# Second attention of a six-stage network: score stacks held twice on the two row halves of TensorE, the split of the row maxima rewritten, and a larger share for GpSimd

## The chip, the cores and the metric

One core of one Trainium2 chip runs the whole program in one launch. The metric is the device time of that launch in microseconds (us); smaller is better.

## What is computed

The reference is a network on x of 4 x 1024 tokens with 128 features: half a step of a 4-expert feed-forward, a causal attention, half a step of feed-forward again, half a step of an 8-expert feed-forward, a second attention, and half a step of the 8-expert feed-forward. The change touches the second attention alone. It has 16 heads of 8 features and adds two attentions over the same scores:

```python
S = einsum('bhnd,bhmd->bhnm', Q, K) / dh ** 0.5
W_tau = softmax(S, axis=-1)
W_sigma = 1.0 / ((1.0 + abs(S) / b_) ** 2 + t_ ** 2)
W_sigma = W_sigma / W_sigma.sum(axis=-1)
f = 0.5 * (W_tau @ V) + 0.5 * (W_sigma @ V)
```

In the kernel the sequence has 1024 positions and there are 4 x 16 = 64 pairs of batch and head; "head" below means such a pair. fp32 accuracy of the scores comes from bfloat16 matmuls: q and k are each split in three bfloat16 parts, and products of parts are summed along the contraction.

## The kernel before, in words

The second attention is the function `attend_both`. A head has 8 tiles of 128 rows; a **slot** is two of them (`i` = 0 and 1), so a head has 4 slots (`PER`) and the stage 256. In slot j each engine works on several slots at once, at fixed lags: maxima of slot j, absolute values and squares of slot j-4 (`LS`), exponentials of slots j-6 (`LT`, `LE`), weighting of V for slot j-7 (`LP`). There is no scheduler: the order on each engine is the order in which `body` is written, and semaphores tie the engines together.

Per slot and engine:

- **TensorE (PE)**: for i = 0 and 1 a score tile of 128 x 1024 into `pm`, one into `pb`, one into `pa` (function `scores`, L1442, two matmuls of 512 columns each; K stack and Q stack of 9 products x 8 features = 72 rows, taken as 96 rows, or 128 with the three rows that carry minus the maximum for `pb`). Then `weigh` (L1458): 4 matmuls of 512 columns per tile, side by side on four column groups of 32.
- **VectorE (DVE)**: for each i the row maximum of `pm` (L1604), and clearing the sign bit of `pa` into `sg` (L1612). Then the square step (a + b) * a on columns 800 to 1023 of both tiles (L1628, `scalar_tensor_tensor` with `sg` as both tensor inputs).
- **GpSimd (POOL)**: the same square step on columns 0 to 799 (`CUT` = 25/32 of 1024), in three instructions: the sum for the first 8 columns (`EDGE`, L1397), the sum for the rest (L1399), the product (L1402). It starts when both sign-cleared tiles are there.
- **ScalarE (ACT)**: exp of `pb` twice (L1524), then logarithm (L1539) and exponential (L1543) that turn the square into the sigma weights.

Once per head, in the first slot of the next head (`j % PER == 0`; **head slot** below), DVE also does the **split** (function `part`): the 128 x 8 maxima become three bfloat16 parts of minus the maximum, in five small instructions L1560, L1564, L1567, L1569, L1571, placed between the large ones. PE turns them (L1494), DVE copies them to `rows` one slot later (L1622), SP sends them by DMA into the Q stack (L1418), and `pb` needs them one slot after that. The output of an earlier head (L1583, L1588, L1592) is done in the head slot too. POOL copies `parh` and `Vh` for the next head there (L1386, L1388). SP loads the stacks of the head after the next one in 6 DMAs (`load_stacks`, L974 and L975).

Of the kernel before, what the change touches and what calls it, by code (L numbers as in the profile page):

```python
# [32 lines left out]
RING = 4  # L33
SIGN_OFF = 0x7FFFFFFF
# [1269 lines left out]

def attend_both(nc, tag, V, F, par, qd, kd, ident, stacks, cleared):
# [10 lines left out]
    EDGE = 8  # L1316
    CUT = 25 * T // 32
    with ExitStack() as ctx:
# [29 lines left out]
        HEAD_LOADS = 16 * STACK_DMAS  # L1348
# [22 lines left out]
        with nc.Block() as block:  # L1371

            @block.gpsimd
            def _(pool):
# [3 lines left out]
                def body(it, j):  # L1378
# [4 lines left out]
                    if (j - LS) % PER == 0:  # L1383
                        if some(h, 2):
                            pool.wait_ge(pv_done, PER * (h - 1))
                        nc.gpsimd.tensor_copy(parh[:, ((j - LS) // PER) % RING, :], par[:, h, :])\  # L1386
                            .then_inc(par_ready, 1)
# [13 lines left out]
                    pool.wait_ge(shift_done, 2 * s + 2)  # L1401
# [6 lines left out]
            def _(sp):  # L1408
                sp.wait_ge(cleared, CLEARS)

                def load(h, r, wait):
                    if wait:
                        sp.wait_ge(tau_mm, TT * (h - RING) + TT)
                    load_stacks(sp, Q[r], K[r], qd, kd, h, stack_in[r])
# [22 lines left out]
            def _(pe):  # L1437
                pe.wait_ge(identb_ready, 1)

                def scores(out, lhsT, rhs, t, rows_, sem):  # L1440
                    for lo in range(0, T, CH):
                        last = nc.tensor.matmul(out[:, lo:lo + CH], lhsT[0:rows_, t * P:(t + 1) * P],  # L1442
                                                rhs[0:rows_, lo:lo + CH], start=True, stop=True)
# [20 lines left out]
                def body(it, j):  # L1464
# [325 lines left out]
```

## Time and profile before

| what | value |
|---|---|
| time, median of 3 runs | 3559.43 us (3557.44 to 3564.81) |
| span of the profiled execution | 3560.9 us |
| busy share of the span: PE, DVE, ACT, POOL | 83%, 82%, 69%, 52% |
| the second attention, first to last head (POOL's first and last `parh` copy) | 1476.8 to 3213.3 us |
| granted TensorE clock, mean | 0.911 of full |

The profile gives for the profiled execution its span; no separate time is shown for it, and the span lies within the three runs' times. Busy shares are means over stages with different limits, so the second attention has to be read by itself. In rows of the timeline a duration runs from an instruction's start to its last write, and the next one may start some 0.07 us before that; a start is when the instruction was taken up, not when it got its first data.

### The profile page before, as it was taken

What the parts mean: (1) busy time and instruction counts of PE and PEld (TensorE: products, weight loads), DVE (VectorE), ACT (ScalarE), POOL (GpSimd) and SP (SyncE); (2) the same over time, 40 slices, a digit from 0 to 9 for tenths busy, and PEclk for the clock granted to TensorE, in tenths of its full rate; (3) what the DMA queues carried; (4) which work ended last, traced back from release to release, by engine and by line L of the source; (5) the groups of instructions that cost most, each with busy time, mean ns of one, the idle gap of its engine ahead of it and who ended that gap; (6) DMA issues with size and microseconds to landing.
All of it is one profiled execution on the core that took longest, in us unless ns stands there. A gap on an engine that the chain in (4) does not pass through costs nothing. (4 is left out here: it accounts for less than half of the span.)

```text
span 3560.9 us, 64791 instructions
## 1 busy us (share of the span) xinstructions
PE 2950.8 (83%) x19824; PEld 1285.0 (36%) x19824; DVE 2905.9 (82%) x5109; ACT 2449.7 (69%) x3005; POOL 1854.7 (52%) x1283
## 2 busy tenths in 40 slices
PE   4987999999798897478788788878878888885699
PEld 3753444444576454222222222222222222222455
DVE  5996777777499666699999999999999999997665
ACT  3973656656497453288888888888888888885354
POOL 3210000000121444188888888888888888885354
PEclk9987999999799798699999989998999999897699
DMA  3002111110000000200000000000000000000000
GB/s 88 0 0 99 35 33 33 32 33 25 1 1 0 1 1 0 81 14 11 10 13 10 10 11 13 10 10 12 12 10 11 13 10 10 12 5 1 1 13 12
DMA packets 48969, 62.18 MB, mean 17 GB/s; under 512 B 8464, under 2 KB 27920, under 8 KB 48880
## 3 DMA queue, kind: packets, MB, share of 16 engines
q1 hardware_dynamic: 48880, 61.08, 5.5%
q8 instruction: 45, 0.74, 0.1%
q14 instruction: 44, 0.36, 0.0%
HBM read 45.60 MB, written 14.68 MB: 17 GB/s over the span
## 5 line engine op out<-in xcount | busy, mean ns | idle before, releaser
L1402 POOL TENSOR_TENSOR a_sg<-a_sg,a_shifted 128x1600 f32<-128x1600 f32 x256 | 923.0, 3606 | 21.4
L1524 ACT ACTIVATE a_pt<-a_pb 128x1024 f32<-128x1024 f32 x512 | 526.5, 1028 | 310.0 <-PE a_pb L1442 308.8
L1604 DVE TENSOR_REDUCE a_mx<-a_pm 128x1 f32<-128x1024 f32 x512 | 622.5, 1216 | 89.3 <-PE a_pm L1442 81.6
L1612 DVE TENSOR_SCALAR a_sg<-a_pa 128x1024 int32<-128x1024 int32 x512 | 617.3, 1206 | 29.0 <-PE a_pa L1442 28.3
L1287 DVE TENSOR_REDUCE a_mx<-a_pm 128x1 f32<-128x512 f32 (+3 forms) x768 | 404.0, 550 | 158.6 <-PE a_pm L1126 150.4
L1458 PE MATMUL a_po<-a_pt,a_Vh 128*32 128x512 f32 x2048 | 527.8, 639 | 2.2 <-ACT a_sg L1543 2.2
L1458 PE MATMUL a_po<-a_sg,a_Vh 128*32 128x512 f32 x2048 | 527.7, 639 | 0.0
L1214 ACT ACTIVATE a_pt<-a_pb 128x512 f32<-128x512 f32 (+3 forms) x768 | 337.2, 501 | 268.6 <-PE a_pb L1140 96.4
L1539 ACT ACTIVATE a_sg<-a_sg,a_parh 128x2048 f32<-128x2048 f32 x256 | 514.0, 2008 | 0.0
L1543 ACT ACTIVATE a_sg<-a_sg 128x2048 f32<-128x2048 f32 x256 | 492.5, 1924 | 0.0
L1399 POOL TENSOR_SCALAR a_shifted<-a_sg,a_parh 128x1584 f32<-128x1584 f32 x256 | 453.4, 1771 | 0.1
L1442 PE MATMUL a_pm<-all_K,all_Q 96*128 96x512 bf16 x1024 | 345.4, 422 | 129.0 <-DVE a_mx L1604 111.9
L1442 PE MATMUL a_pa<-all_Q,all_K 96*128 96x512 bf16 x1024 | 341.6, 418 | 41.2 <-DVE a_sg L1612 28.9
L1442 PE MATMUL a_pb<-all_Q,all_K 128*128 128x512 bf16 x1024 | 342.2, 418 | 8.2 <-ACT a_pt L1524 8.2
L1071 POOL COPY a_Vh<-all_V 128x72 f32 (+1 forms) x64 | 13.9, 252 | 567.9 <-PE a_po L1158 567.9
L1123 PE MATMUL a_pm<-all_K,all_Q 96*128 96x512 bf16 (+3 forms) x768 | 258.5, 342 | 24.6 <-DMA all_K<-k_parts 21.4
L1137 PE MATMUL a_pb<-all_Q,all_K 128*128 128x512 bf16 (+3 forms) x768 | 247.1, 327 | 7.9 <-ACT a_pt L1214 7.4
L1628 DVE SCALAR_TENSOR_TENSOR a_sg<-a_sg,a_parh 128x448 f32<-128x448 f32 x256 | 222.1, 867 | 8.9
L1158 PE MATMUL a_po<-a_pt,a_Vh 128*32 128x512 f32 (+3 forms) x1536 | 224.1, 497 | 0.0
L614 ACT ACTIVATE f_sg<-f_psg 128x512 f32<-128x512 f32 x176 | 105.1, 597 | 167.9 <-PE f_psg L573 166.9
L1397 POOL TENSOR_TENSOR a_shifted<-a_sg,a_parh 128x16 f32<-128x16 f32 x256 | 75.9, 297 | 272.6 <-DVE a_sg L1612 247.7
L327 POOL TENSOR_TENSOR f_hidl<-f_hid,f_hidh 128x512 f16<-128x512 f32 x64 | 76.3, 1193 | 263.3 <-ACT f_hid L398 263.3
(244 smaller groups left out, 6061.9 us busy)
## 6 DMA issues: line engine op xcount, KB each, us to landing
all_Q<-q_parts SPq DMA_DIRECT2D x384, 48.0 KB
all_K<-k_parts SPq DMA_DIRECT2D x384, 48.0 KB
q_parts<-p_parts SPq DMA_DIRECT2D x16, 384.0 KB, 2.6
k_parts<-p_parts SPq DMA_DIRECT2D x16, 384.0 KB, 2.6
all_Q<-a_rows SPq DMA_DIRECT2D x128, 6.0 KB
out_dram<-all_X SPq DMA_DIRECT2D x8, 256.0 KB, 2.3
sw_raw<-in_f_We_dram SPq DMA_DIRECT2D x1, 1024.0 KB, 7.1
sw_raw<-in_f_w_gP_dram SPq DMA_DIRECT2D x1, 704.0 KB, 11.0
```

The source lines that it names most:

```text
L1123: last = nc.tensor.matmul(out[:, 0:hi - lo], Q[r][0:96, t * P:(t + 1) * P], K[r][0:96, lo:hi], start=True, stop=not diagonal)
L1214: nc.scalar.activation(pt[:, u, t % 2, lo:hi], pb[:, y % 3, lo % CH:CH], ACT.Exp, scale=SC)\
L1287: nc.vector.tensor_reduce(mx[:, j % 2, half, u, t:t + 1], pm[:, y % 3, 0:min(CH, (t + 1) * P - half * CH)], AX.X, ALU.max).then_inc(max_re ...
L1399: nc.gpsimd.tensor_scalar(shifted[:, :, EDGE:CUT], buf[:, :, EDGE:CUT], b2, 1.0, ALU.add, ALU.mult)\
L1402: nc.gpsimd.tensor_tensor(buf[:, :, 0:CUT], buf[:, :, 0:CUT], shifted[:], ALU.mult)\
L1442: last = nc.tensor.matmul(out[:, lo:lo + CH], lhsT[0:rows_, t * P:(t + 1) * P], rhs[0:rows_, lo:lo + CH], start=True, stop=True)
L1458: last = nc.tensor.matmul(po[32 * q:32 * q + 32, :], Vh[:, ((j - LP) // PER) % 2, t, :], wts[:, i, half * CH:(half + 1) * CH], start=(t == ...
L1524: nc.scalar.activation(pt[(j - LT) % 4][:, i, :], pb[:], ACT.Exp, scale=SC)\
L1539: nc.scalar.activation(buf[:], buf[:], ACT.Ln, bias=parh[:, ((j - LE) // PER) % RING, 1:2]).then_inc(ln_done, 1)
L1543: nc.scalar.activation(buf[:], buf[:], ACT.Exp, scale=-1.0).then_inc(sig_done, 1)
L1604: nc.vector.tensor_reduce(mx[:, (j // PER) % 2, t:t + 1], pm[:], AX.X, ALU.max)\
L1612: nc.vector.tensor_scalar(sg[(j - LS) % 4][:, i, :].bitcast(I32), pa[:].bitcast(I32), SIGN_OFF, None, ALU.bitwise_and).then_inc(abs_done, 1)
```

## The change

- Both operands of the scores are held twice, on partitions 0 to 50 and 64 to 114. Six products of parts are kept instead of nine (48 rows, and 3 more for the maxima: 51). The two matmuls of a score tile (columns 0 to 511, 512 to 1023) read the two copies, so that they lie on different row halves of the array.
- The loads of a head are 12 DMAs instead of 6, and the maxima are sent by 2 DMAs instead of 1. The rows of ones are set by two memsets on POOL in the stage before (`load_sharpness`).
- The split is four `tensor_tensor` instructions with both inputs in SBUF. The maxima are now taken negated, so the sign is not changed in the split. The fifth place is empty.
- `CUT` goes from 25/32 to 27/32; the `EDGE` instruction on POOL is gone, and a nop carries POOL's wait for the sign-cleared tiles. `parh` is copied one head ahead.

```diff
+HALF = P // 2
+QPARTS = (0, 0, 0, 1, 1, 2)
+PAIRS = len(QPARTS) * DH
+MAX_ROW = PAIRS
...
+def load_halves(eng, Q, K, qd, kd, g, sem):
+
+    for base in (0, HALF):
+        row = base
+        for part, times in ((0, 3), (1, 2), (2, 1)):
+            rows = slice(row, row + times * DH)
+            eng.dma_start(Q[rows, :], qd[part, g].unsqueeze(0).broadcast_to([times, DH, T])).then_inc(sem, 16)
+            eng.dma_start(K[rows, :], kd[0:times, g]).then_inc(sem, 16)
+            row += times * DH
...
+def set_ones(eng, Ks, sem):
+
+    for base in (0, HALF):
+        eng.memset(Ks[base + 32:base + HALF, 0:RING, :], 1.0).then_inc(sem, 1)
...
-    EDGE = 8
-    CUT = 25 * T // 32
+    CUT = 27 * T // 32
...
                     if some(s):
                         pool.wait_ge(sq_pool, s)
+                    pool.wait_ge(par_ready, h + 1)
                     pool.wait_ge(abs_done, 2 * s + 2)
-                    pool.wait_ge(par_ready, h + 1)
+                    pool.nop(nofuse=True)
...
-                    nc.gpsimd.tensor_tensor(shifted[:, :, 0:EDGE], buf[:, :, 0:EDGE],
-                                            b2.unsqueeze(2).broadcast_to([P, 2, EDGE]), ALU.add).then_inc(shift_done, 1)
-                    nc.gpsimd.tensor_scalar(shifted[:, :, EDGE:CUT], buf[:, :, EDGE:CUT], b2, 1.0, ALU.add, ALU.mult)\
+                    nc.gpsimd.tensor_scalar(shifted[:], buf[:, :, 0:CUT], b2, 1.0, ALU.add, ALU.mult)\
                         .then_inc(shift_done, 1)
...
                     sp.wait_ge(rows_sb, h + 1)
-                    sp.dma_start(Q[r][ONES_ROW:ONES_ROW + SPLIT, :].rearrange("s (t n) -> s t n", n=P),
-                                 rows[:]).then_inc(rows_in[r], 16)
+                    for base in (0, HALF):
+                        sp.dma_start(Q[r][base + MAX_ROW:base + MAX_ROW + SPLIT, :]
+                                     .rearrange("s (t n) -> s t n", n=P), rows[:]).then_inc(rows_in[r], 16)
...
                 def scores(out, lhsT, rhs, t, rows_, sem):
-                    for lo in range(0, T, CH):
-                        last = nc.tensor.matmul(out[:, lo:lo + CH], lhsT[0:rows_, t * P:(t + 1) * P],
-                                                rhs[0:rows_, lo:lo + CH], start=True, stop=True)
+                    for base, lo in ((0, 0), (HALF, CH)):
+                        last = nc.tensor.matmul(out[:, lo:lo + CH], lhsT[base:base + rows_, t * P:(t + 1) * P],
+                                                rhs[base:base + rows_, lo:lo + CH], start=True, stop=True)
                     last.then_inc(sem, 1)
...
-                        nc.vector.tensor_scalar(neg3[:, 0, :], top, -1.0, None, ALU.mult).then_inc(chain, 1)
-                    else:
-                        dve.wait_ge(chain, 4 * h + n)
+                        nc.vector.tensor_tensor(neg3[:, 0, :], low, low, ALU.max).then_inc(chain, 1)
                     if n == 1:
-                        nc.vector.scalar_tensor_tensor(rem[:], top, -1.0, neg3[:, 0, :], ALU.mult, ALU.subtract)\
-                            .then_inc(chain, 1)
+                        dve.wait_ge(chain, 3 * h + 1)
+                        nc.vector.tensor_tensor(neg3[:, 1, :], low, neg3[:, 0, :], ALU.subtract).then_inc(chain, 1)
                     if n == 2:
-                        nc.vector.tensor_copy(neg3[:, 1, :], rem[:]).then_inc(chain, 1)
+                        nc.vector.tensor_tensor(rem[:], low, neg3[:, 0, :], ALU.subtract).then_inc(chain, 1)
                     if n == 3:
-                        nc.vector.tensor_tensor(rem[:], rem[:], neg3[:, 1, :], ALU.subtract).then_inc(chain, 1)
-                    if n == 4:
-                        nc.vector.tensor_copy(neg3[:, 2, :], rem[:]).then_inc(parts_ready, 1)
+                        dve.wait_ge(chain, 3 * h + 3)
+                        nc.vector.tensor_tensor(neg3[:, 2, :], rem[:], neg3[:, 1, :], ALU.subtract)\
+                            .then_inc(parts_ready, 1)
...
-                            nc.vector.tensor_reduce(mx[:, (j // PER) % 2, t:t + 1], pm[:], AX.X, ALU.max)\
-                                .then_inc(max_red, 1)
+                            nc.vector.tensor_reduce(mx[:, (j // PER) % 2, t:t + 1], pm[:], AX.X, ALU.max,
+                                                    negate=True).then_inc(max_red, 1)
```

DVE's order in the head slot, in the steady part of the stage, of the kernel before (`a_neg` and `a_rem` are the tiles of the split, `a_mx` the maxima, `a_sg` the absolute scores; the first row ends the slot before):

```order
L1628 SCALAR_TENSOR_TENSOR a_sg<-a_sg,a_parh 128x2x224
L1560 TENSOR_SCALAR a_neg<-a_mx 128x8
L1604 TENSOR_REDUCE a_mx<-a_pm 128x1
L1564 SCALAR_TENSOR_TENSOR a_rem<-a_mx,a_neg 128x8
L1583 RECIPROCAL a_rz<-a_ptr 128x16
L1612 TENSOR_SCALAR a_sg<-a_pa 128x1024
L1567 CAST a_neg<-a_rem 128x8
L1588 TENSOR_TENSOR a_fw<-a_ptr,a_rz 128x128
L1604 TENSOR_REDUCE a_mx<-a_pm 128x1
L1569 TENSOR_TENSOR a_rem<-a_rem,a_neg 128x8
L1592 TENSOR_TENSOR all_XNT<-a_fw 128x8x8
L1612 TENSOR_SCALAR a_sg<-a_pa 128x1024
```

And the same place on DVE in the changed kernel:

```order
L1652 SCALAR_TENSOR_TENSOR a_sg<-a_sg,a_parh 128x2x160
L1586 TENSOR_TENSOR a_neg<-a_mx 128x8
L1628 TENSOR_REDUCE a_mx<-a_pm 128x1
L1589 TENSOR_TENSOR a_neg<-a_mx,a_neg 128x8
L1607 RECIPROCAL a_rz<-a_ptr 128x16
L1636 TENSOR_SCALAR a_sg<-a_pa 128x1024
L1591 TENSOR_TENSOR a_rem<-a_mx,a_neg 128x8
L1612 TENSOR_TENSOR a_fw<-a_ptr,a_rz 128x128
L1628 TENSOR_REDUCE a_mx<-a_pm 128x1
L1594 TENSOR_TENSOR a_neg<-a_rem,a_neg 128x8
L1616 TENSOR_TENSOR all_XNT<-a_fw 128x8x8
L1636 TENSOR_SCALAR a_sg<-a_pa 128x1024
```

The four small instructions stand where the first four stood; the fifth is gone from before the next square step.

POOL's order in one slot in the loop, of the kernel before:

```order
L1392 REGISTER_ALU
L1393 ISA
L1397 TENSOR_TENSOR a_shifted<-a_sg,a_parh 128x2x8
L1399 TENSOR_SCALAR a_shifted<-a_sg,a_parh 128x2x792
L1402 TENSOR_TENSOR a_sg<-a_sg,a_shifted 128x2x800
```

And in the changed kernel:

```order
L1426 REGISTER_ALU
L1427 TENSOR_TENSOR a_sg<-a_sg,a_shifted 128x2x864
L1420 ISA
L1424 TENSOR_SCALAR a_shifted<-a_sg,a_parh 128x1728
L1426 REGISTER_ALU
```

POOL's large sum now follows its waits directly, with no short instruction ahead of it.

## Rows read from the trace of the kernel before

**Rows 1.** Stretch, us; busy PE, PEld, DVE, ACT, POOL (instructions); clock; DMA; GB/s
```profile
1800.00:2400.00 600.00, 487.76 (x2590) 139.03 (x2578) 562.72 (x644) 502.93 (x376) 505.70 (x311) 0.92 0.04 11
```
**Rows 2.** The `parh` copies, one per head: all of them by line, then three in time
```profile
L1386 POOL COPY a_parh<-all_par x64: 174/180/199, 1476.8 to 3213.3; 128x2 f32 x60, 128x2 f32<-128x2 f32 x4
...
2397.63 0.18 POOL L1386 COPY a_parh<-all_par 128x2 f32 x1
...
2425.78 0.18 POOL L1386 COPY a_parh<-all_par 128x2 f32 x1
...
2452.30 0.18 POOL L1386 COPY a_parh<-all_par 128x2 f32 x1
```
**Rows 3.** Timeline, DVE at a head boundary: start us, duration us, instruction
```profile
2445.79 1.22 DVE L1628 SCALAR_TENSOR_TENSOR a_sg<-a_sg,a_parh 128x448 f32<-128x448 f32 x1
2446.94 0.18 DVE L1560 TENSOR_SCALAR a_neg<-a_mx 128x8 bf16<-128x8 f32 x1
2447.07 1.23 DVE L1604 TENSOR_REDUCE a_mx<-a_pm 128x1 f32<-128x1024 f32 x1
2448.21 0.46 DVE L1564 SCALAR_TENSOR_TENSOR a_rem<-a_mx,a_neg 128x8 f32<-128x8 f32 x1
...
2448.76 1.16 DVE L1612 TENSOR_SCALAR a_sg<-a_pa 128x1024 int32<-128x1024 int32 x1
2449.84 2.55 DVE L1567 CAST a_neg<-a_rem 128x8 bf16<-128x8 f32 x1
...
2452.50 1.21 DVE L1604 TENSOR_REDUCE a_mx<-a_pm 128x1 f32<-128x1024 f32 x1
...
2455.08 0.74 DVE L1628 SCALAR_TENSOR_TENSOR a_sg<-a_sg,a_parh 128x448 f32<-128x448 f32 x1
```
**Rows 4.** Timeline, POOL over the same stretch
```profile
2442.92 3.61 POOL L1402 TENSOR_TENSOR a_sg<-a_sg,a_shifted 128x1600 f32<-128x1600 f32 x1
2446.76 0.34 POOL L1397 TENSOR_TENSOR a_shifted<-a_sg,a_parh 128x16 f32<-128x16 f32 x1 [0.23 <-POOL a_sg L1402]
2447.07 1.58 POOL L1399 TENSOR_SCALAR a_shifted<-a_sg,a_parh 128x1584 f32<-128x1584 f32 x1
2448.74 3.62 POOL L1402 TENSOR_TENSOR a_sg<-a_sg,a_shifted 128x1600 f32<-128x1600 f32 x1
...
2455.13 0.22 POOL L1397 TENSOR_TENSOR a_shifted<-a_sg,a_parh 128x16 f32<-128x16 f32 x1 [2.46 <-DVE a_sg L1612]
2455.32 1.95 POOL L1399 TENSOR_SCALAR a_shifted<-a_sg,a_parh 128x1584 f32<-128x1584 f32 x1
```
**Rows 5.** Timeline, the stage after the attention: DVE
```profile
3284.45 2.32 DVE L937 TENSOR_TENSOR o_t<-o_rs 128x8 f32<-128x8 f32 x1
3286.80 2.26 DVE L938 TENSOR_TENSOR o_t<-o_t,o_ve 128x8 f32<-128x8 f32 x1
```
**Rows 6.** Timeline, the same stretch: POOL
```profile
3283.47 3.27 POOL L902 TENSOR_TENSOR o_y<-o_y,all_lw 128x1024 f32<-128x1024 f32 x1 [2.96 <-DVE o_y L942]
3286.70 2.33 POOL L898 TENSOR_TENSOR all_X<-all_X,all_lb 128x1024 f32<-128x1024 f32 x1
```
**Rows 7.** PE alone, two stretches: us, PE busy, granted clock, DMA share, GB/s
```profile
2402.50:2409.30 6.80, 6.71 (x25) 0.54 0.07 23
2409.30:2425.80 16.50, 14.68 (x87) 1.00 0.03 9
```
**Rows 8.** Timeline, PE at the lower clock: first and last group of one slot's weighing
```profile
2405.27 1.06 PE L1458 MATMUL a_po<-a_pt,a_Vh 128*32 128x512 f32 x2
...
2407.83 1.06 PE L1458 MATMUL a_po<-a_pt,a_Vh 128*32 128x512 f32 x2
```
**Rows 9.** SP issuing one head's six loads: the first and the last
```profile
2404.93 0.76 SPq L974 DMA_DIRECT2D all_Q<-q_parts  x1
...
2409.36 0.73 SPq L975 DMA_DIRECT2D all_K<-k_parts  x1
```
**Rows 10.** POOL's earlier memset of ones, by line: duration ns min/median/max
```profile
L986 POOL MEMSET all_K<- x1: 6924/6924/6924, 25.2 to 25.2; 32x8192 bf16 x1
```

More of the change, by code:

```diff
@@ L1347, in attend_both @@
             m.sem(x) for x in ("taumm", "tauexp", "vh", "par", "pv", "osb", "oturned", "fd", "rz", "weighed"))
-        HEAD_LOADS = 16 * STACK_DMAS
+        HEAD_LOADS = 16 * HALVES_DMAS
         def at(it, j, lag):
@@ L1385, in body @@
                             pool.wait_ge(pv_done, PER * (h - 1))
-                        nc.gpsimd.tensor_copy(parh[:, ((j - LS) // PER) % RING, :], par[:, h, :])\
-                            .then_inc(par_ready, 1)
+                        if not some(h):
+                            nc.gpsimd.tensor_copy(parh[:, 0, :], par[:, h, :]).then_inc(par_ready, 1)
+                        if not (isinstance(h, int) and h + 1 >= HEADS):
+                            nc.gpsimd.tensor_copy(parh[:, ((j - LS) // PER + 1) % RING, :], par[:, h + 1, :])\
+                                .then_inc(par_ready, 1)
                         nc.gpsimd.tensor_copy(Vh[:, ((j - LS) // PER) % 2, :, 0:DH + 1], V[:, h, :, :])\
@@ L1408, in _ @@
             def _(sp):
-                sp.wait_ge(cleared, CLEARS)
+                sp.wait_ge(cleared, CLEARS + 2)
                 def load(h, r, wait):
@@ L1469, in body @@
                     if st is not None and (j - LT) % PER == 0:
-                        pe.wait_ge(rows_in[rt], 16 * (it + (j - LT) // PER // RING + 1))
+                        pe.wait_ge(rows_in[rt], 32 * (it + (j - LT) // PER // RING + 1))
                     for i in range(2):
@@ L1474, in body @@
                                 pe.wait_ge(max_red, 2 * sm + i)
-                            scores(pm, Q[rm], K[rm], 2 * (j % PER) + i, 96, max_mm)
+                            scores(pm, Q[rm], K[rm], 2 * (j % PER) + i, PAIRS, max_mm)
                         if st is not None:
@@ L1478, in body @@
                                 pe.wait_ge(tau_exp, 2 * st + i)
-                            scores(pb, K[rt], Q[rt], 2 * ((j - LT) % PER) + i, P, tau_mm)
+                            scores(pb, K[rt], Q[rt], 2 * ((j - LT) % PER) + i, PAIRS + SPLIT, tau_mm)
                         if ss is not None:
@@ L1482, in body @@
                                 pe.wait_ge(abs_done, 2 * ss + i)
-                            scores(pa, K[rs], Q[rs], 2 * ((j - LS) % PER) + i, 96, abs_mm)
+                            scores(pa, K[rs], Q[rs], 2 * ((j - LS) % PER) + i, PAIRS, abs_mm)
                         if i and sp_ is not None:
@@ L1554, in part @@
                         return
-                    h, top = head(it, j, 1), mx[:, ((j - 1) // PER) % 2, :]
+                    h, low = head(it, j, 1), mx[:, ((j - 1) // PER) % 2, :]
                     if n == 0:
@@ L1619, in body @@
                             if some(h):
-                                dve.wait_ge(rows_in[r], 16 * (it + ((j - 2) // PER - 1) // RING + 1))
+                                dve.wait_ge(rows_in[r], 32 * (it + ((j - 2) // PER - 1) // RING + 1))
                             nc.vector.tensor_copy(rows[:], ptr[:].bitcast(BF16)[0:SPLIT * TT, 0:P])\
@@ L1633, in attend_both, with load_sharpness @@
         m.clear_sems()
-def load_sharpness(nc, tag, par, beta, t):
+def load_sharpness(nc, tag, par, beta, t, Ks, ones_set):
     with ExitStack() as ctx:
@@ L1643, in load_sharpness, with _ @@
         with nc.Block() as block:
+            @block.gpsimd
+            def _(pool):
+                set_ones(pool, Ks, ones_set)
             @block.sync
@@ L1736, in program @@
             lambda: ln_transposed(nc, "n5", X, XNT, ident, add_to_x=True),
-            lambda: load_sharpness(nc, "s5", par, layer["a1_"]["beta"], layer["a1_"]["t"]),
+            lambda: load_sharpness(nc, "s5", par, layer["a1_"]["beta"], layer["a1_"]["t"], stacks[1], cleared),
             lambda: project(nc, "p5", XNT, V, qd, kd, a1, a1_in, True, 2.0),
```

5 lines of the change are left out of this document (3 added, 2 removed).

## The prediction

> **What bounds the kernel now.** I read the windows first, then the copies that mark the heads, then the timeline of a head boundary, since the change is all in the second attention and most of it happens once per head. In the middle of that stage DVE is busy 562.7 of 600 us, PE 488, ACT 503, POOL 506 [rows 1]: no engine is full. The `parh` copies give the pitch of a head: (3213.3 - 1476.8) / 63 = 27.56 us, and single heads take either 28.15 us or 26.5 us (2397.63 to 2425.78, 2425.78 to 2452.30) [rows 2]. POOL's two large instructions need 3.61 + 1.58 us per slot when nothing holds them [rows 4], so with the gaps some 23 of the 26.5 us; the rest is lost at the head boundary. The reader should see in [rows 3, 4] that **DVE and POOL hold each other up**. A DVE instruction with two SBUF tensors as inputs, or a cast from SBUF to SBUF, is not done while a POOL instruction runs; whichever comes second waits for the whole of the other:
>
> - L1628 starts at 2445.79 under L1402, which ends at 2446.53; it ends at 2447.01, 0.48 later, though a free one takes 0.74 [rows 3, 4].
> - L1564 (8 columns, two inputs) takes 0.46 us and ends 0.02 us after L1399. The cast L1567 starts at 2449.84 and ends at 2452.39, 0.03 us after L1402 [rows 3, 4]: 2.4 us lost, per head.
> - The other way round, L1399 takes 1.95 instead of 1.58 us when L1628 has started just before it [rows 4].
>
> While DVE waits in the cast, POOL runs dry for 2.46 us, since its next tile needs both L1612 of that slot [rows 4]. In the other slots POOL's pitch is L1402 end to L1402 end: 2446.53 to 2452.36, 5.83 us, in which L1628 and L1397 take the 0.54 us between 2446.53 and 2447.07. So POOL and DVE in turn set the end; PE does so only while its clock is at 1.2 GHz.
>
> **The change, part by part.** I count from the end of POOL's product before the boundary (0 = 2446.53).
>
> *Split.* This kind of instruction stands in the next stage: `tensor_tensor` on 128 x 8 fp32, L937 with the same tile as both inputs, L938 with two. They take 2.32 and 2.26 us [rows 5], and end 0.03 us after POOL's L902 and L898 [rows 6]. So the new instructions are held up like the cast. There is more: L937 gets through between two POOL instructions because it was already waiting; L938, taken up at 3286.80, just after L898 (3286.70), waits for all of it. Now the first instruction of the split. Before, the short L1397 stood ahead of L1399: L1560 (taken up at 0.41) waited for it and went in ahead of L1399, done at 0.59 [rows 3, 4]. Now L1628 (320 instead of 448 columns, 128 / 448 of 0.467 us less, taken from its 0.48 after release) ends at 0.35, the first split instruction is taken up at 0.28, and POOL's sum stands ready at 0.23, where L1397 stood. I take it that POOL goes first.
>
> *POOL.* The product scales with columns: 3.61 x 27 / 25 = 3.89. The sum: 1.58 x 1728 / 1584 = 1.72. L1397 goes. Pitch in a plain slot: 0.23 + 1.72 + 0.09 + 3.89 = 5.93 (before 5.83).
>
> *The head slot, now.* POOL: sum 0.23 to 1.95, product 2.04 to 5.93. DVE: first split instruction done at 1.98; maximum from 1.93; second split instruction taken up 1.14 later, at 3.07, waits for the product, done at 5.96. From there the distances of [rows 3], with the reciprocal between: sign clearing 6.05, third split instruction 7.13 (POOL is dry, no wait), second maximum 7.40 (before 2452.50, which is 5.97), square step 2.58 after that (2452.50 to 2455.08), at 9.98 (before 8.55). POOL's sum ends 2.20 after that at 12.18 (before 2.19: 2455.08 to 2457.27), its product at 12.27 + 3.89 = 16.16. Two plain slots: 16.16 + 2 x 5.93 = **28.02 us per head**. DVE keeps up in these: from one square step to the next it needs 0.6 and four large instructions at 1.1 to 1.2, 5.2 us; with the copy of `rows` 5.4.
>
> *PE.* Before, at a clock of 0.54, the head takes 28.15 instead of 26.5 [rows 2, 7]; PE had been idle while DVE stood in the cast. Half of the score columns now run beside the other half, so the six pairs of a slot cost the time of six matmuls instead of twelve; at 2.4 GHz this was hidden behind POOL and stays hidden. At 1.2 GHz 512 columns are 0.43 us, and the four groups of weighing, 0.85 apart, 3.4 [rows 8]: a slot needs 6 x 0.43 + 3.4 = 6.0 instead of 12 x 0.43 + 3.4 = 8.6 us, against POOL's 5.93. Between 0 and 1.7 us per head I take 0.2, near the lower end, since DVE and ACT have slack after the head slot.
>
> *Edits with nothing to pay.* SP has 12 loads at 0.88 (2404.93 to 2409.36 is five steps) = 10.6 us instead of 5.3, and one more row DMA of 0.9 [rows 9], of 28 us; the loads are for the head after the next. The second row DMA comes some 1 us later at `pb`; PE's slack per slot covers it. ACT is busy 503 of 600 us [rows 1], 23.1 per head. If POOL did not cover, each would show as a wait of under 1 us.
>
> *Ones.* The memsets write 2 x 4096 columns; 8192 took 6.92 us [rows 10]. The stage before lasts about 6 us, so up to 3.5 us are added; I take 3.
>
> **Sum:** 64 x (28.02 + 0.2 - 27.56) = 42, and 3: +45 us on the span of 3560.9 or the median of 3559.4, which differ by less than the runs do. **3605 us.**
>
> The Trainium skill ("VectorE: DVE Perf Modes", section "Mode 2×_2P") says that the mode with both read ports is for instructions with one source, and that `tensor_tensor` cannot use it. Read by itself it would let the split escape from POOL, and the time would be that of the first rival below, 3400 instead of 3605. Its page "SBUF — State Buffer", section "Who interferes with whom", has the other half, two SBUF inputs against a POOL instruction that reads; with that one the trace agrees, at 2.32 and 2.26 us for an instruction of 128 x 8. "TensorEngine Tiling (Array Packing)", section "Key Properties", says that a change of tiling mode drains TensorE; no row prices it.
>
> **The rivals.**
>
> 1. *The two-input form is not held up.* Then neither the 1.5 nor the 2.7 us of waiting arise, and DVE never falls behind: 4 x 5.93 = 23.7, with POOL's two copies at the boundary and small losses 25 us per head, 64 x 2.5 = 160 us less, 3400. Against it: [rows 5, 6], at the same shape. For it: nothing here. 7%.
> 2. *The first split instruction gets in ahead of POOL's sum*, because POOL's own taking up costs 0.1 us more than at L1397. Then it is done at 0.4, the maximum runs 0.35 to 1.5, the second slips in between sum and product (as L1564 did), and the third waits for the product as the cast did. The end is as before plus POOL's columns: 26.53 + 4 x 0.12 = 27.0 us, and the low clock costs less than before (27.0 to 27.5): 64 x (-0.56 to -0.06) + 3 = 3526 to 3558. It is decided by 0.1 us between two starts. 20%.
> 3. *PE at the lower clock for long stretches*, since it has less to do and longer gaps. A slot is then the chain pair, maximum, sign clearing, pair, weighing: 0.63 + 1.2 + 1.2 + 0.43 + 3.4 = 6.9 us, and with the 2.7 us of waiting at the boundary 30.3 us per head if the clock stays low all the time, 3738; half the time, some 3670. For: the clock falls behind each gap [rows 7]. Against: it comes back within 7 us. 13%.
>
> The forecast, all held up, 3580 to 3640, has 60%.
>
> **How the numbers follow.** The range 3525 to 3670 takes in the forecast, nearly all of rival 2 and the lower part of rival 3. A measurement of this kernel can tell about 0.2%, 7 us. Faster: rival 1 and most of 2, 25%. Same: 8%. Slower: 67%.
>
> **What would show it.** In the changed profile: the first split instruction about 1.7 us long and ending with POOL's sum, the second about 2.9 us and ending with POOL's product, third and fourth 0.15 us; POOL idle some 4 us per head ahead of its sum; the square step on DVE some 1.3 us in the other slots; `parh` copies 28.2 us apart. Short split instructions, or a first one of 0.2 us, would prove rival 1 or 2; a granted clock well under 0.9 rival 3.

## The result, and the profile after

The changed kernel takes **3597.24 us** (3593.86 to 3601.18, 4 runs) against 3561.51 (3557.44 to 3564.81, 4 runs) for the kernel before: a ratio of 1.010, 95% interval 1.0088 to 1.0112. It is slower by 36 us; forecast were 3605, that is +45. The span of the profiled execution is 3599.4 us, 38.5 more than before. The size fits; the way to it does not. I begin with the windows, in the middle of the second attention (columns as in [rows 1]):

```profile
1800.00:2400.00 600.00, 439.93 (x2531) 100.11 (x2533) 549.69 (x607) 495.70 (x369) 503.06 (x217) 0.80 0.05 15
```

PE does its work in 440 us instead of 488, and its granted clock has gone from 0.92 to 0.80 [rows 1]. Every engine is less busy than before, and none is full.

Next the `parh` copies, by line, then five in time (compare [rows 2]):

```profile
L1412 POOL COPY a_parh<-all_par x63: 176/184/204, 1479.3 to 3225.4; 128x2 f32 x60, 128x2 f32<-128x2 f32 x3
...
2366.38 0.19 POOL L1412 COPY a_parh<-all_par 128x2 f32 x1
2395.98 0.18 POOL L1412 COPY a_parh<-all_par 128x2 f32 x1
2425.34 0.18 POOL L1412 COPY a_parh<-all_par 128x2 f32 x1
2452.47 0.18 POOL L1412 COPY a_parh<-all_par 128x2 f32 x1
2479.60 0.18 POOL L1412 COPY a_parh<-all_par 128x2 f32 x1
```

These four heads take 29.60, 29.36, 27.13 and 27.13 us. Of the 61 steady heads 43 lie at 27.0 to 27.2 and 18 between 28.2 and 29.8; their mean is (3225.4 - 1533.1) / 61 = 27.74, where 1533.1 is the second copy. The kernel before, counted from its second copy at 1533.5 in the same way, has (3213.3 - 1533.5) / 62 = 27.09. The difference, 0.65 x 61 = 40 us, is the whole of the 38.5. All of what the mean has above the short heads (27.10 on average) comes from the 18 long ones. In the kernel before, 42 heads take up to 27.15 us (26.57 on average) and 20 take 28.0 to 28.3.

Which form does the head take? The four split instructions, by line (duration ns min/median/max, first and last start):

```profile
L1586 DVE TENSOR_TENSOR a_neg<-a_mx x64: 152/177/1568, 1503.9 to 3249.2; 128x8 bf16<-128x8 f32 x64
...
L1589 DVE TENSOR_TENSOR a_neg<-a_mx,a_neg x64: 156/467/3473, 1505.8 to 3249.4; 128x8 bf16<-128x8 f32 x64
...
L1591 DVE TENSOR_TENSOR a_rem<-a_mx,a_neg x64: 142/2794/2803, 1507.0 to 3252.1; 128x8 f32<-128x8 f32 x64
...
L1594 DVE TENSOR_TENSOR a_neg<-a_rem,a_neg x64: 147/150/153, 1508.2 to 3255.0; 128x8 bf16<-128x8 f32 x64
```

I had forecast 1.7, 2.9, 0.15 and 0.15 us. The first takes 0.15 to 0.18 in 62 of 64 heads. In 44 heads the second takes 0.47 (but for one) and the third 2.8: the pattern of my second rival. In 19 others the second takes 2.3 to 3.5, as I had it for the second, and the third 0.14 to 0.15. First the more frequent form, in the head of 27.13 us that ends at 2479.60; DVE (compare [rows 3]):

```profile
2472.76 1.33 DVE L1652 SCALAR_TENSOR_TENSOR a_sg<-a_sg,a_parh 128x320 f32<-128x320 f32 x1
2474.01 0.18 DVE L1586 TENSOR_TENSOR a_neg<-a_mx 128x8 bf16<-128x8 f32 x1
2474.11 1.21 DVE L1628 TENSOR_REDUCE a_mx<-a_pm 128x1 f32<-128x1024 f32 x1
2475.25 0.47 DVE L1589 TENSOR_TENSOR a_neg<-a_mx,a_neg 128x8 bf16<-128x8 f32 x1
...
2476.89 2.79 DVE L1591 TENSOR_TENSOR a_rem<-a_mx,a_neg 128x8 f32<-128x8 f32 x1
```

and POOL (compare [rows 4]):

```profile
2469.86 3.88 POOL L1427 TENSOR_TENSOR a_sg<-a_sg,a_shifted 128x1728 f32<-128x1728 f32 x1
2474.00 1.71 POOL L1424 TENSOR_SCALAR a_shifted<-a_sg,a_parh 128x1728 f32<-128x1728 f32 x1 [0.25 <-POOL a_sg L1427]
2475.79 3.86 POOL L1427 TENSOR_TENSOR a_sg<-a_sg,a_shifted 128x1728 f32<-128x1728 f32 x1
...
2482.52 1.99 POOL L1424 TENSOR_SCALAR a_shifted<-a_sg,a_parh 128x1728 f32<-128x1728 f32 x1 [2.56 <-DVE a_sg L1636]
```

POOL's sum and the first split instruction are taken up 0.01 us apart, 2474.00 and 2474.01, and the split instruction is done at 2474.19; the sum takes its usual 1.71. The second slips in between sum and product, and the third stands from 2476.89 until the product has ended at 2479.65. POOL then runs dry for 2.56 us, as it did for 2.46 behind the cast [rows 4].

Now the other form, at the end of a head of 27.08 us, DVE and then POOL:

```profile
1667.94 0.18 DVE L1586 TENSOR_TENSOR a_neg<-a_mx 128x8 bf16<-128x8 f32 x1
1669.31 1.22 DVE L1628 TENSOR_REDUCE a_mx<-a_pm 128x1 f32<-128x1024 f32 x1 [1.18 <-PE a_pm L1468]
1670.45 3.13 DVE L1589 TENSOR_TENSOR a_neg<-a_mx,a_neg 128x8 bf16<-128x8 f32 x1
...
1669.72 3.84 POOL L1427 TENSOR_TENSOR a_sg<-a_sg,a_shifted 128x1728 f32<-128x1728 f32 x1
...
1677.74 2.01 POOL L1424 TENSOR_SCALAR a_shifted<-a_sg,a_parh 128x1728 f32<-128x1728 f32 x1 [3.87 <-DVE a_sg L1636]
```

PE had been weighing at the lower clock (its groups of that slot start 0.85 us apart), so the scores came late and the maximum waited 1.18 us for them. The second split instruction is therefore taken up 0.73 us after the start of POOL's product instead of ahead of it, and stands until the product has ended at 1673.56. The sign clearing behind it is late, and POOL is dry for 3.87 us. In all 19 heads of this form that maximum had waited 0.5 to 2.0 us for PE; in the other 45 heads it had done so once. The heads that follow the 19 (18 can be counted) are exactly the 18 long ones, 28.2 to 29.8 us; all 43 that follow another form take 27.0 to 27.2.

The scores do overlap. PE at full clock (first matmul's start to the end of both):

```profile
2467.58 0.39 PE L1468 MATMUL a_pm<-all_K,all_Q 48*128 48x512 bf16 x2
2467.81 0.38 PE L1468 MATMUL a_pb<-all_Q,all_K 51*128 51x512 bf16 x2
```

And two such pairs in the kernel before:

```profile
2414.29 0.60 PE L1442 MATMUL a_pm<-all_K,all_Q 96*128 96x512 bf16 x2
2414.73 0.60 PE L1442 MATMUL a_pb<-all_Q,all_K 128*128 128x512 bf16 x2
```

The pairs stand 0.23 and 0.44 us apart. And here is PE's clock, in windows of PE alone (us, PE busy, clock, DMA share, GB/s):

```profile
2420.00:2422.00 2.00, 0.78 (x4) 1.00 0.00 0
2422.00:2424.00 2.00, 1.25 (x6) 0.58 0.00 0
2424.00:2426.00 2.00, 2.00 (x16) 0.57 0.00 0
2426.00:2428.00 2.00, 1.15 (x9) 1.00 0.00 0
2428.00:2430.00 2.00, 0.42 (x4) 0.78 0.00 0
2430.00:2432.00 2.00, 1.91 (x10) 0.50 0.00 0
```

Thin stretches (0.78 and 0.42 of 2 us) are each followed by a fall to 1.2 GHz. Counted in windows of 1 us over the stage, the clock falls 2.3 times in a head instead of 0.95 times, and is low for some 11 us of each head instead of 4.4. DVE's waits for `pm` grow: 151.3 us before L1628 over the program, against 81.6 at L1604 of before.

### The profile page after: what moved, and what is told of

Its sections match the earlier page's. It is cut to its first block and busy times, and to the rows that moved or that the text cites. A ratio compares the mean times of both kernels' runs of the same rounds, so it can differ in the third digit from the quotient of the medians.

```text
span 3599.4 us, 65422 instructions
## 1 busy us (share of the span) xinstructions
PE 2831.1 (79%) x19824; PEld 1175.0 (33%) x19824; DVE 2908.7 (81%) x5045; ACT 2457.9 (68%) x3005; POOL 1886.3 (52%) x1029
## 5 line engine op out<-in xcount | busy, mean ns | idle before, releaser
L1427 POOL TENSOR_TENSOR a_sg<-a_sg,a_shifted 128x1728 f32<-128x1728 f32 x256 | 991.1, 3871 | 21.4
L1628 DVE TENSOR_REDUCE a_mx<-a_pm 128x1 f32<-128x1024 f32 x512 | 621.5, 1214 | 151.3 <-PE a_pm L1468 151.3
L1484 PE MATMUL a_po<-a_pt,a_Vh 128*32 128x512 f32 x2048 | 722.4, 845 | 0.8 <-ACT a_sg L1569 0.8
L1484 PE MATMUL a_po<-a_sg,a_Vh 128*32 128x512 f32 x2048 | 722.1, 845 | 0.0
L1424 POOL TENSOR_SCALAR a_shifted<-a_sg,a_parh 128x1728 f32<-128x1728 f32 x256 | 480.0, 1875 | 288.3 <-DVE a_sg L1636 231.6
L1468 PE MATMUL a_pm<-all_K,all_Q 48*128 48x512 bf16 x1024 | 225.3, 437 | 289.2 <-DVE a_mx L1628 267.4
L1468 PE MATMUL a_pa<-all_Q,all_K 48*128 48x512 bf16 x1024 | 230.7, 447 | 166.5 <-DVE a_sg L1636 159.1
L1468 PEld LDWEIGHTS a_pm<-all_K,all_Q 48*128 48x128 bf16 x1024 | 50.2, 94 | 610.1 <-DVE a_mx L1628 399.5
L1468 PE MATMUL a_pb<-all_Q,all_K 51*128 51x512 bf16 x1024 | 220.3, 427 | 29.1 <-ACT a_pt L1550 27.4
L1484 PEld LDWEIGHTS a_po<-a_pt,a_Vh 128*32 128x32 f32 x2048 | 123.4, 137 | 343.0 <-issue 343.0
L1652 DVE SCALAR_TENSOR_TENSOR a_sg<-a_sg,a_parh 128x320 f32<-128x320 f32 x256 | 218.6, 854 | 13.0
```

What stands on the lines that cost most here:

```text
L1424: nc.gpsimd.tensor_scalar(shifted[:], buf[:, :, 0:CUT], b2, 1.0, ALU.add, ALU.mult)\
L1427: nc.gpsimd.tensor_tensor(buf[:, :, 0:CUT], buf[:, :, 0:CUT], shifted[:], ALU.mult)\
L1468: last = nc.tensor.matmul(out[:, lo:lo + CH], lhsT[base:base + rows_, t * P:(t + 1) * P], rhs[base:base + rows_, lo:lo + CH], start=True, ...
L1484: last = nc.tensor.matmul(po[32 * q:32 * q + 32, :], Vh[:, ((j - LP) // PER) % 2, t, :], wts[:, i, half * CH:(half + 1) * CH], start=(t == ...
L1628: nc.vector.tensor_reduce(mx[:, (j // PER) % 2, t:t + 1], pm[:], AX.X, ALU.max, negate=True).then_inc(max_red, 1)
```

## The experiments

Each was timed beside the kernel before on the same chip (medians of before 3560 to 3561 us). "Head" is the mean pitch from the second `parh` copy on, "clock" the granted clock between 1800 and 3000 us (0.92 before, 0.80 after).

**1. The new split alone** (the diff of `part` and of the maxima above, on the kernel before).

> The kernel before with the new split alone (negated maxima, four two-input instructions); columns, EDGE and score stacks as before. Theory A (the split is held up by POOL as the cast was, its third instruction by the product): within 5 us of the kernel before, third instruction about 2.5 us. Theory B (two-input instructions escape POOL): 60 x 2.4 = 140 us faster. Theory C (as the prediction had it, the first one also waits for POOL's sum): some 1.5 us per head, 90 us slower; here the short POOL instruction is still there, so C expects its effect only in the changed kernel.

3572.16 us, ratio 1.0025 (1.0012 to 1.0037); head 27.31, clock 0.91. The wait that the cast had now sits in the third split instruction:

```profile
L1565 DVE TENSOR_TENSOR a_rem<-a_mx,a_neg x64: 149/2532/2547, 1505.7 to 3222.2; 128x8 f32<-128x8 f32 x64
```

The first two take 0.17 and 0.27 us on average. One instruction fewer gains nothing (the kernel is 12 us slower, where I had allowed 5), since the instruction that lands on POOL's product is again one that reads two SBUF tiles.

**2. The halves alone** (stacks, loads, memsets and `scores` of the change; old split, `EDGE`, `CUT` 25/32).

> The kernel before with the score stacks of 51 rows held twice, the doubled loads and row sends and the memsets; split, EDGE and columns as before. Theory A: pairs of score matmuls start 0.22 us apart instead of 0.44, but PE is hidden behind POOL and DVE at the full clock, and what the shorter work saves in slots at the lower clock is lost again by more such slots: between -15 and +10 us, granted clock of the stage near 0.8. Rival: the halves are a gain by themselves (less work at the lower clock), 30 us or more faster.

3658.84 us, ratio 1.028 (1.026 to 1.0301); head 28.57, clock 0.80. Both expectations were wrong: it is 98 us slower. DVE waits on PE, in the timeline:

```profile
2325.34 0.68 DVE L1656 SCALAR_TENSOR_TENSOR a_sg<-a_sg,a_parh 128x448 f32<-128x448 f32 x1
2327.38 1.22 DVE L1632 TENSOR_REDUCE a_mx<-a_pm 128x1 f32<-128x1024 f32 x1 [1.35 <-PE a_pm L1470]
```

PE does less (852 of 1200 us busy, before 978) and the kernel loses 98 us. Most heads take 28.45 or 29.5 us. The same form as in the change is at work: the second instruction of the split (L1592 here) takes over 2 us in 48 of 64 heads, and the maximum ahead of it had waited for PE in each of the 48. The heads after these take 28.98 on average, the others 27.17. No head is free of falls of the clock; even the two shortest, of 26.0 us, have three stretches at 1.2 GHz.

**3. `CUT` alone**, on the kernel before.

```diff
-    CUT = 25 * T // 32
+    CUT = 27 * T // 32
```

> The kernel before with CUT 27/32 alone. Theory A: POOL's sum and product are longer by 0.14 and 0.28 us, DVE's square step shorter by 0.13, which POOL waits for; so a head is longer by up to 4 x 0.28 = 1.1 us, and by less where POOL waits for DVE: 30 to 70 us slower. Rival (DVE sets the end): 4 x 0.13 us per head, 30 us faster.

3602.04 us, ratio 1.0118 (1.01 to 1.0136); head 27.77, clock 0.92.

**4. The change with that line taken back.**

> The changed kernel with CUT back at 25/32. Theory A: POOL's pitch falls from 5.91 to about 5.6, a head from 27.1 to about 26.0, 60 us faster than the changed kernel, so some 25 us faster than before. Rival (the share of POOL does not matter since DVE sets the end): as the changed kernel or slower.

3600.03 us, ratio 1.012 (1.0093 to 1.0148); head 27.63, clock 0.82. I had expected 60 us less than the changed kernel; it is the same. So the larger share for POOL costs 41 us on the kernel before and nothing within the change: the parts do not add (12 + 98 + 41 against 36; `EDGE` was not taken out of the kernel before by itself). The traces show why. The second split instruction is held by POOL's product in none of the 64 heads of the kernel before and of experiment 3, in 1 of experiment 1, in 19 of the change and in 36 of experiment 4. With the smaller share the heads that follow an unheld one take 26.77 us instead of 27.10, but there are far fewer of them (26 instead of 43).

**5. Halves without overlap** (halves alone, both matmuls of a pair on the lower copy).

```diff
-                    for base, lo in ((0, 0), (HALF, CH)):
+                    for base, lo in ((0, 0), (0, CH)):
```

> The halves-only kernel (2.8% slower than before) with both matmuls of a score tile on the lower copy, so that they run one after the other: PE has twice the array time for scores, all loads, row sends and memsets stay. Theory D (the halves lose through the clock: the shorter work leaves PE idle more, the granted clock falls in more slots, and DVE then waits for PE): faster than the halves-only kernel by 60 to 100 us, back at 3560 to 3580, stage clock back to about 0.9. Rival E (the doubled loads, row sends or 51-row stacks themselves cost it): no faster than the halves-only kernel, 3650 or more.

3794.77 us, ratio 1.0663 (1.0646 to 1.0681); head 30.73, clock 0.78. I had expected 3560 to 3580 and a clock of 0.9 if idleness of PE were the cause. PE is busy 1029 of 1200 us and the clock does not come back (some of that busy time is the lower clock itself, at which the same matmul takes twice as long). That PE is merely too idle is not the whole of it.

**6. A split that never reads two SBUF tiles.** On the change: the maxima are first copied to PSUM, and all subtractions have that copy as one input. The instructions are also moved: all of them stand near the end of the slot, behind the second maximum.

```diff
+                        nc.vector.tensor_scalar(top, low, 1.0, None, ALU.mult).then_inc(chain, 1)
...
+                        nc.vector.tensor_tensor(left, top, neg3[:, 0, :], ALU.subtract).then_inc(chain, 1)
+                        nc.vector.tensor_tensor(neg3[:, 1, :], top, neg3[:, 0, :], ALU.subtract).then_inc(chain, 1)
```

> The changed kernel with the split after a copy of the maxima into PSUM: five small instructions with at most one SBUF tensor input and PSUM at one end, later in the head slot. Theory A (port between DVE and POOL holds up the split): each takes under 0.25 us; the hold-up moves to L1616, the sum of the output with two SBUF inputs, which now meets POOL's product (up to 2.5 us once per head); so little gain, 0 to 60 us. Rival F (what is lost at the boundary is not this hold-up but the number of instructions or PE): no gain and L1616 still 0.2 us.

3570.64 us, ratio 1.0031 (1.002 to 1.0043); head 27.28, clock 0.78. The split instructions all fall to 0.15 to 0.17 us, and the wait moves to the next DVE instruction with two SBUF inputs, the sum of the output (0.21 in the change, 1.20 here in the middle):

```profile
L1617 DVE TENSOR_TENSOR all_XNT<-a_fw x64: 215/1196/1754, 1559.2 to 3259.0; 128x64 f32 x60, 128x64 f32<-128x64 f32 x4
```

That is not all: the head slot's square step, also an instruction with two SBUF inputs, takes 1.94 to 1.96 us in 59 of 61 heads here, and 0.55 to 0.57 in every head of the change. It comes back under 11.

**7. The same, and the output's sum with one input in PSUM.**

```diff
+                        for q, to in ((slice(2, 4), fw[:, :, 2:4, :]), (slice(0, 2), o[:, :, 0:2, 0:DH])):
...
-                                                fw[:, :, 0:2, :].rearrange("p c s d -> p s c d"),
+                                                o[:, :, 0:2, 0:DH].rearrange("p c s d -> p s c d"),
```

> The same and also the output's sum with one input in PSUM (one instruction more per head). Theory A: nothing but the square step has two SBUF inputs in the head slot any more; POOL never runs dry, a head is 4 x 5.91 and POOL's two copies, 24.2 us, if the clock allows: 3360 to 3430. Theory D adds: with the halves PE has half of the time nothing to do, so the clock stays near 0.8 and slots at 1.2 GHz cost some of it: 3400 to 3480. Rival F: 3590 or more.

3468.47 us, ratio 0.9739 (0.9721 to 0.9758); head 25.66, clock 0.85, as expected with a low clock.

**8. The same two edits on the kernel before**: the diffs of experiments 6 and 7, with 72-row stacks, `EDGE` and 25/32 as they were (and -1.0 as the factor of the copy to PSUM, since the maxima are not negated here).

> The kernel before with the same two edits (split and output sum without a second SBUF input), score stacks, columns and EDGE as before. Theory A: a head is 4 x 5.83 and the copies, 23.7 to 24.3 us, 3380 to 3400. Theory D: clock well above the halves kernel's, 0.95 or more, since nothing makes PE stand still at the boundary, and so faster than the same split in the changed kernel. Rival: at this pitch PE with 12 matmuls one after the other is too long (its busy time would be over 80% of the slot at full clock) and DVE waits for it: 3450 or more.

**3358.29 us** (3356.82 to 3359.95), ratio **0.9435** (0.9419 to 0.9451): 202 us better than before, 239 better than the change. Every head takes 23.7 to 23.9 us and the clock is 1.00 (expected were 3380 to 3400 and 0.95 or more):

```profile
1800.00:2400.00 600.00, 511.20 (x2943) 149.08 (x2945) 587.74 (x754) 571.85 (x429) 573.53 (x353) 1.00 0.04 13
```

DVE and POOL are now busy 98% and 96% of the time. The output's sum with one input in PSUM passes under POOL's product, where experiment 6 had it held for 1.20 us:

```profile
2412.11 0.23 DVE L1593 TENSOR_TENSOR all_XNT<-a_ptr,a_fw 128x64 f32 x1
...
2409.65 3.60 POOL L1402 TENSOR_TENSOR a_sg<-a_sg,a_shifted 128x1600 f32<-128x1600 f32 x1
```

It takes 0.21 to 0.23 us in the 62 of 64 heads in which it starts under the product.

**9. The same with 48 rows instead of 96** in the matmuls for `pm` and `pa` (this leaves out a third of the products in the maxima and the absolute values).

```diff
-                            scores(pm, Q[rm], K[rm], 2 * (j % PER) + i, 96, max_mm)
+                            scores(pm, Q[rm], K[rm], 2 * (j % PER) + i, 48, max_mm)
...
-                            scores(pa, K[rs], Q[rs], 2 * ((j - LS) % PER) + i, 96, abs_mm)
+                            scores(pa, K[rs], Q[rs], 2 * ((j - LS) % PER) + i, 48, abs_mm)
```

> e8_before_psum_sum with 48 instead of 96 rows of the stacks in the matmuls for the maxima and the absolute values (a third of the products is left out of these two; pb keeps all): same instructions, same columns, same array time, same DMAs, only fewer rows of the array in use. Theory G (the clock that is granted goes by how much of the array works, so that 48 rows for the same time count for less than 96): granted clock below 1.00, 0.8 to 0.95 in the stage, and the time 30 to 250 us over e8. Rival H (it is the doubled loads and row sends or the tiles in the other row half that cost it in e5): clock 1.00 and time within 5 us of e8.

3365.91 us, ratio 0.9446 (0.9429 to 0.9462); head 24.01, clock 1.00. The number of rows in `pm` and `pa` does not set the clock here.

**10. Experiment 7 with every pair of scores issued twice.**

```diff
-                    for base, lo in ((0, 0), (HALF, CH)):
+                    for base, lo in ((0, 0), (HALF, CH), (0, 0), (HALF, CH)):
```

> e7_split_psum_sum (row halves, split and output sum without a second SBUF input, CUT 27) with every pair of score matmuls issued twice into the same place, the second time with the same result: 51 rows in both halves for the array time of before. Theory G: the clock comes back to nearly 1.00 and the heads to the 23.97 us that e7's undisturbed heads take, so 80 to 110 us FASTER than e7 though PE does more, about 3370. Rival H or any cost of PE's own time: slower than e7, 3470 or more.

3570.39 us, ratio 1.0018 (1.0008 to 1.0027), 102 us slower than experiment 7; head 27.17, clock 0.87. PE is busy 1021 of 1200 us, as much as in experiment 8 (1022), and still loses its clock in 59 of 61 heads. I had expected about 3370 if array time brought the clock back. What lengthens these heads came out in the next pair.

**11. Experiment 8 without `EDGE`** (POOL's sequence of the change, `CUT` 25/32), and **12. the same with 24/32**.

```diff
+                    pool.nop(nofuse=True)
...
-                    nc.gpsimd.tensor_tensor(shifted[:, :, 0:EDGE], buf[:, :, 0:EDGE],
-                                            b2.unsqueeze(2).broadcast_to([P, 2, EDGE]), ALU.add).then_inc(shift_done, 1)
-                    nc.gpsimd.tensor_scalar(shifted[:, :, EDGE:CUT], buf[:, :, EDGE:CUT], b2, 1.0, ALU.add, ALU.mult)\
+                    nc.gpsimd.tensor_scalar(shifted[:], buf[:, :, 0:CUT], b2, 1.0, ALU.add, ALU.mult)\
```

> e8_before_psum_sum with POOL's short EDGE instruction gone and the nop in its place, CUT 25. The split needs no gap in POOL's work any more, and POOL sets the pitch (23.85 us per head): 0.25 us less per slot, down to where DVE (about 22.7 us per head) is as long: 22.7 to 23.2 us, 3290 to 3320.

> The same with CUT 24. If POOL still sets the pitch in e11, 0.1 us per slot less, 25 us faster than e11; if DVE does (square step of 512 columns, 0.07 us more per slot), 10 to 20 us slower. I expect DVE.

3556.28 us (3536.2 to 3559.56), ratio 0.9978 (0.9964 to 0.9993), and 3558.25, ratio 0.9987 (0.9972 to 1.0002); clock 0.88 and 0.87. I had expected 3290 to 3320, and 10 to 20 us more or 25 less for 24/32. Leaving out a POOL instruction of 0.2 to 0.3 us costs 198 us, the whole of the gain. (The edit also puts in the nop and turns two waits round; these were not tried by themselves.) The timelines tell the reason. Experiment 8 at a head's change, POOL then DVE:

```profile
2413.62 0.22 POOL L1397 TENSOR_TENSOR a_shifted<-a_sg,a_parh 128x16 f32<-128x16 f32 x1
2413.82 2.06 POOL L1399 TENSOR_SCALAR a_shifted<-a_sg,a_parh 128x1584 f32<-128x1584 f32 x1
...
2413.74 0.68 DVE L1629 SCALAR_TENSOR_TENSOR a_sg<-a_sg,a_parh 128x448 f32<-128x448 f32 x1
2414.66 1.22 DVE L1605 TENSOR_REDUCE a_mx<-a_pm 128x1 f32<-128x1024 f32 x1 [0.24 <-PE a_pm L1442]
```

Experiment 11, the same place:

```profile
2422.86 1.60 POOL L1397 TENSOR_SCALAR a_shifted<-a_sg,a_parh 128x1600 f32<-128x1600 f32 x1 [0.62 <-DVE a_sg L1611]
...
2422.87 0.17 DVE L1567 TENSOR_TENSOR a_neg<-a_ptr,a_neg 128x8 bf16<-128x8 f32 x1
2422.97 1.96 DVE L1627 SCALAR_TENSOR_TENSOR a_sg<-a_sg,a_parh 128x448 f32<-128x448 f32 x1
2424.85 1.21 DVE L1603 TENSOR_REDUCE a_mx<-a_pm 128x1 f32<-128x1024 f32 x1
...
2426.12 1.03 PE L1440 MATMUL a_pm<-all_K,all_Q 96*128 96x512 bf16 x2 [1.40 <-DVE a_mx L1603]
```

POOL is released by DVE's last sign clearing of the slot, and DVE comes to its square step three small split instructions later. With `EDGE`, POOL first does 0.2 us of something else, DVE's square step gets in ahead of the large sum and takes 0.68. Without it the sum is taken up 0.11 us sooner than the square step, which then waits it out: 1.96. The split's last instruction, with one of its inputs in PSUM, is taken up 0.01 us after the sum and takes its usual 0.17. The next maximum starts 1.88 us after the square step did, instead of 0.92, PE waits 1.40 us for it, and the clock falls. Windows of experiment 11 (columns as in [rows 1]):

```profile
2418.00:2426.00 8.00, 5.13 (x30) 1.42 (x29) 7.90 (x16) 7.05 (x6) 7.22 (x6) 0.98 0.00 0
2426.00:2433.00 7.00, 6.88 (x25) 1.66 (x26) 4.36 (x6) 4.06 (x3) 4.99 (x3) 0.53 0.08 24
2433.00:2452.00 19.00, 16.24 (x94) 4.76 (x91) 18.22 (x24) 17.36 (x14) 15.95 (x9) 1.00 0.02 7
```

For 7 us PE is full at 0.53 and DVE is busy only 4.36 of them. These 2.6 us and the 1.28 of the held square step cover the 3.4 us that a head is longer than in experiment 8 (27.25 for 23.85). Experiment 11 loses in 60 of its 62 counted heads (27.25 us on average), and its two heads in which the square step was not held (taken up 0.06 us before the sum and 0.01 after) took 23.03 and 23.51, with no fall of the clock; all of the 60 have one. In experiment 10 the square step takes 1.94 to 2.00 us in 59 of 61 heads, and in experiment 6 it was held as often: there too `EDGE` is gone. So experiment 10 says little on PE; the square step was held in it, and in experiments 8 and 9 it was held in none of 62 heads.

Experiment 7 has both forms within one kernel. A head boundary that loses, then one that doesn't, DVE and POOL each:

```profile
2179.46 1.94 DVE L1655 SCALAR_TENSOR_TENSOR a_sg<-a_sg,a_parh 128x320 f32<-128x320 f32 x1
...
2179.35 1.71 POOL L1424 TENSOR_SCALAR a_shifted<-a_sg,a_parh 128x1728 f32<-128x1728 f32 x1 [1.96 <-DVE a_sg L1639]
...
2204.28 0.55 DVE L1655 SCALAR_TENSOR_TENSOR a_sg<-a_sg,a_parh 128x320 f32<-128x320 f32 x1
...
2204.44 1.96 POOL L1424 TENSOR_SCALAR a_shifted<-a_sg,a_parh 128x1728 f32<-128x1728 f32 x1
```

Over its 61 steady heads: in 30 the square step is taken up 0.08 to 0.11 us after the sum, takes 1.94 to 1.96 us, and the head 26.96 on average; in 31 it is taken up between 0.17 us before the sum and together with it, takes some 0.55, and the head 24.41 (23.95 to 24.91 but for two, 25.87 and 27.37). No square step was taken up between 0.00 and 0.08 us after the sum. This also shows what the output's sum was worth in experiment 7: its heads with a held square step take 26.96, against 27.30 of those in experiment 6. Most of the 102 us between the two experiments comes from the 31 heads whose square step got through. In experiment 11, with both edits and the square step held in 60 heads, the mean head is 27.13, against 27.09 of the kernel before: nothing is gained.

## Why the prediction was right, and where its steps failed

**The size** of the result was right (3605 for 3597), the sign too, but by errors that cancel, which is luck:

- **"I take it that POOL goes first" failed.** Worked out were starts of 0.23 for POOL's sum and 0.28 for the split instruction after the end of the product; in the trace they are 0.26 and 0.27 after 2473.74, and although the split instruction is the later one it is not held. The rest of that term, 28.02 us per head, falls with it: 43 of 61 heads take 27.0 to 27.2, as the second rival had it (27.0). This was the step I had called decided by 0.1 us, and I gave the wrong side 60%. The second split instruction did wait for the product in 19 of 64 heads, as forecast, but because PE was late and not because POOL's sum had gone first.
- **The clock's cost was mis-sized**: I took 0.2 us per head. The mean is 27.74 where 43 heads take 27.10, so it is about 0.6, inside the bounds of 0 to 1.7. I had looked for it in PE's own time per slot. It comes about through the order on DVE: the maximum waits for PE, the second split instruction misses its place ahead of the product, and the next one or two heads take 28.2 to 29.8. (No head of the changed kernel is free of stretches at 1.2 GHz, so that some cost within the 27.10 is not excluded.) The clock in the stage is 0.80. My argument against the third rival, that the clock comes back within 7 us, was true, but it falls again within the same head. Experiment 2 shows the price of the halves on their own: 98 us.
- **The reference of the sum was wrong**: 27.56 us was a mean that took in the start-up interval of 57 us (1476.8 to 1533.5). The steady heads of before take 27.09. Against that, an honest count by my steps would have given 64 x (28.22 - 27.09) + 3 = 75 us, too much by two times. The second rival suffered from the same reference: with 27.09 its 27.0 to 27.5 us per head give 61 x (-0.09 to 0.41) + 3, that is -2 to +28 us, and with the measured 0.6 for the clock 61 x (27.0 + 0.6 - 27.09) + 3 = 34, close to the 38.5 of the trace. The chances did not add up either: the forecast (60%) and the third rival (13%) are both slower, but "slower" got 67%.
- **The split is held up like the cast**: right. The third of its instructions takes 2.8 us (2.5 in experiment 1) or, in 19 heads, the second 2.3 to 3.5; the first rival is gone. The Trainium skill ("SBUF — State Buffer", section "Who interferes with whom") says that a DVE instruction with two SBUF inputs contends with a GpSimd instruction that reads SBUF; the trace agrees, with these numbers. The same section of the Trainium skill says that issue order decides who blocks; experiment 7 agrees, where the square step was held in each of the 30 heads in which it came 0.08 to 0.11 us after the sum, while in the changed kernel the first split instruction came 0.01 to 0.08 us after the sum in 55 heads and was not held.
- **POOL's columns**: the sum was forecast at 1.72 and took 1.71, the product 3.89 (the formula gives 3.90) and took 3.86 to 3.88. The first `parh` copy comes 2.5 us later (1479.3 for 1476.8), where I had 3 for the memsets of ones.
- **Pairs of scores beside each other**: right, 0.22 us a pair. At full clock they gave nothing, since there PE was not what others waited for.

**What the change was worth part by part** cannot be given as a sum (experiments 1 to 4). What is shown is the way from a lower clock to a longer head. What stays open is why the halves lose the clock, also where PE had little idle time just before. In experiment 5 it falls at 2408.6 us after a stretch (2406 to 2408) in which PE was busy 1.55 of 2 us, while experiment 8 passes a stretch with 1.07 of 2 us (2412 to 2414), and experiment 9 one with 1.44 (2418 to 2420), at full clock. Rows in `pm` and `pa` (experiment 9) and PE's busy share (experiment 5) are excluded as the only reason; the 51 rows of `pb` and the tile position at partition 64 were not tried by themselves. Nor was the combination of the halves with `EDGE` and the edits of experiment 7.

## What to carry to other kernels

Before you shorten work on an engine, list the instructions of its neighbour that can hold it. On DVE each of these with two SBUF inputs, however small, waited for the end of POOL's large instruction when it was taken up inside it (0.01 to 0.08 us after its start was still early enough in the changed kernel). Giving the small ones one input in PSUM was worth 202 us, with more instructions than before, but only where the last one left with two SBUF inputs, the square step, got in ahead of POOL (experiment 8); where it did not, the same edits were worth 5 us (experiment 11). Where two engines are released by the same event, look at the timeline for who is taken up first; a short instruction ahead of the long one can be what lets the other through, and removing it is not free. A faster PE in a loop that others pace is not harmless: at the lower granted clock it can be late for one instruction, and that one then meets what it used to slip past. Judge such an edit by the stage's time, never by PE's busy time.

## What the runs showed of the hardware

- An order settled by less than 0.1 us decides 2.5 to 4 us per head: in experiment 7 heads with the square step first take 24.41 us, the others 26.96; in experiment 11 heads with an unheld square step take 23.3 us, the others 27.25.
- After a stretch with PE busy 5.13 of 8 us the granted clock was 0.53 for 7 us (experiment 11); after the same place in experiment 8, busy 6.17 of 8 us, it stayed at 1.00.
- PE at half the array time per pair came with a lower clock, 0.80 for 0.92, and 2.8% more time (experiment 2, with its doubled loads and row sends); twice the array time without the overlap did not bring the clock back (0.78, experiment 5).
- The order in which two instructions are taken up is not always the order in which they get their data: in 55 heads of the changed kernel the first split instruction came 0.01 to 0.08 us after POOL's sum and was not held (2474.01 and 2474.00 in the rows above). In 6 more it came 0.25 to 0.34 us after a sum that itself stood behind DVE's square step (1.9 to 2.0 us instead of 1.71), and was not held either.
- An instruction with one SBUF and one PSUM input was not held by POOL: the output's sum took 0.21 to 0.23 us under the product (experiment 8), with two SBUF inputs 1.17 to 1.75 (experiment 6, 46 heads).
